# Decoder layer with gated cross-attention on one Trainium2 core: the two products that sum the gates write different partitions of one PSUM bank, and the running maximum reads a copy

## What is computed

```python
itilde = einsum('bsd,hd->bhs', gate_in, Wi_w) + Wi_b
ftilde = einsum('bsd,hd->bhs', gate_in, Wf_w) + Wf_b
csum   = cumsum(log_sigmoid(ftilde), axis=-1)
Fmat   = csum[..., :, None] - csum[..., None, :]
Dtilde = where(tril, Fmat, -inf) + itilde[..., None, :]
max_d  = max(Dtilde, axis=-1)
D      = exp(Dtilde - max_d)
```

## Time and profile before

| | value |
|---|---|
| median of three runs | 1849.2 us (1847.55 to 1849.93) |
| profiled execution, its own time | 1848.03 us |
| its span, first to last instruction | 1846.3 us |
| PE busy | 1772.4 us, 96% of the span |
| PEld busy | 1377.2 us, 75% |
| DVE busy | 1331.0 us, 72% |
| ACT busy | 1151.9 us, 62% |
| POOL busy | 317.5 us, 17% |
| mean granted TensorE clock | 0.982 |

### The profile page before, as it was taken

The page is one execution under the profiler, slowest core; times in us unless marked ns, Lnnn a source line. Parts: engine busy times, 40 slices in busy tenths (PEclk is TensorE's granted clock), DMA queues, the critical chain, the costliest instruction groups (busy, mean ns, idle before and its releaser), DMA issues.

```text
span 1846.3 us, 44235 instructions
## 1 busy us (share of the span) xinstructions
PE 1772.4 (96%) x14172; PEld 1377.2 (75%) x14172; DVE 1331.0 (72%) x3869; ACT 1151.9 (62%) x2634; POOL 317.5 (17%) x301
## 2 busy tenths in 40 slices
PE   5669999999999999999999999999999999999897
PEld 4557777877777787777777777777877777777675
DVE  4677777777777777777777777777777777777752
ACT  1456766666676666667666667666666776666552
POOL 2011211111221111122111212211111221112110
PEclk8889999999999999999999999999999999999998
DMA  5111212221121222112122211212221211221100
GB/s 135 35 39 35 60 37 60 60 59 48 35 60 37 60 60 59 47 37 60 37 60 60 59 38 46 59 38 60 60 58 32 53 49 48 60 60 40 23 15 26
DMA packets 222639, 92.35 MB, mean 50 GB/s; under 512 B 150785, under 2 KB 222082, under 8 KB 222610
## 3 DMA queue, kind: packets, MB, share of 16 engines
q1 hardware_dynamic: 222610, 91.99, 18.9%
HBM read 70.71 MB, written 16.78 MB: 47 GB/s over the span
## 4 chain that ended last, share of the span: by engine, by line
PE 93%; DVE 4%; ACT 1%; issue 1%; DMA 0%; SPq 0%; DVEq 0%; ACTq 0%
PE UA L1460 11%; PE TA L1460 6%; PE UB L1398 6%; PE GT L1460 5%; PE TB L1398 5%; PE PV L1398 5%; PE UA L1423 3%; PE GT L1471 3%; PE TA L1360 3%; PE QQ L1223 3%; PE TA L1398 3%; PE UA L1398 3%; PE DD L1223 2%; PE PV L1506 2%; PE QQ L1491 2%; PE UB L1506 2%
## 5 line engine op out<-in xcount | busy, mean ns | idle before, releaser
L1099 DVE TENSOR_TENSOR C<-qT,QKs 128x512 f32<-128x512 f32 x256 | 178.3, 716 | 181.4 <-ACT qT L759 178.6
L1460 PE MATMUL UA<-W2f,hs_all 128*128 128x256 f32 x1024 | 231.5, 379 | 0.0
L1460 PEld LDWEIGHTS UA<-W2f,hs_all 128*128 128x128 f32 x1024 | 194.4, 190 | 30.5 <-issue 0.2
L618 POOL TENSOR_TENSOR Ng<-HT,gnw_b 128x256 f32<-128x256 f32 x128 | 93.2, 728 | 506.8 <-DVE cden L1112 502.3
L595 POOL TENSOR_TENSOR vc<-vc 128x992 f32<-128x992 f32 x32 | 58.9, 1842 | 632.6 <-DVE ve L871 631.9
L612 POOL TENSOR_TENSOR xg<-x,gnb_b 128x1024 f32<-128x1024 f32 x32 | 75.4, 2356 | 298.2 <-DVE nmx L1065 281.7
L1460 PE MATMUL TA<-W2f,hs_all 128*128 128x256 f32 x512 | 120.8, 379 | 0.0
L1460 PE MATMUL GT<-W2f,hs_all 128*128 128x256 f32 x512 | 115.7, 379 | 0.0
L672 ACT ACTIVATE V<-QQ 128x260 f32<-128x260 f32 x32 | 12.4, 388 | 159.5 <-PE QQ L1255 159.5
L1460 PEld LDWEIGHTS GT<-W2f,hs_all 128*128 128x128 f32 x512 | 94.9, 190 | 11.6
L1460 PEld LDWEIGHTS TA<-W2f,hs_all 128*128 128x128 f32 x512 | 94.9, 190 | 11.3
(11 more groups left out here) (384 smaller groups left out, 5277.8 us busy)
## 6 DMA issues: line engine op xcount, KB each, us to landing
xin<-x SPq DMA_DIRECT2D x32, 512.0 KB, 4.4
xb<-x SPq DMA_DIRECT2D x32, 512.0 KB, 4.1
blocks<-ctx SPq DMA_DIRECT2D x256, 64.0 KB, 2.0
vc<-ctx SPq DMA_DIRECT2D x32, 512.0 KB, 3.6
out<-ot SPq DMA_DIRECT2D x32, 512.0 KB, 3.2
Ev<-xn SPq DMA_DIRECT2D x512, 1.0 KB
hs_all<-L_ffn_W SPq DMA_DIRECT2D x4, 512.0 KB, 9.0
E<-xn SPq DMA_DIRECT2D x128, 16.0 KB
```

The lines of the kernel that those rows point to most:

```text
L618: pool.tensor_tensor(Ng[:, b, :].rearrange("p (k n) -> p k n", k=2), HT[:, b % 2, :, 0:P], gnw_b[:, :].rearrange("p (k n) -> p k n", k=2), ...
L1099: dve.tensor_tensor(C[:, b % 2, :, half], dx[hf].rearrange("p (h i) -> p h i", h=HEADS), QKs[:, b, :, half], ALU.mult)\
L1460: ins = pe.matmul(OB[b][:, 0:D], hs_all[:, k, b * S:(b + 1) * S], W2f[:, k, :], start=(i == 0), stop=(i == KH - 1))
```

## The change

The product with `sel_i` now writes DD[32:64], columns 0 to 127, and the product with `sel_f` still writes DD[0:32], columns 0 to 127: same columns of the bank, different partitions. VectorE's one copy of 32x256 becomes two of 32x128, the first of them from partitions 32 to 63 into partitions 0 to 31 of `acs[:, 1]`. One wait stands behind both. The running maximum reads `acs[:, 1]` in SBUF for both operands.

```diff
-        v_chain = Chain(sem("dve_step"), 42)
+        v_chain = Chain(sem("dve_step"), 43)
...
                 if cross:
                     dve.wait_ge(sel_mm.h, sel_mm.at(it, 1))
-                    link(dve.tensor_copy(acs[:, 0:2, :].rearrange("p a n -> p (a n)"), DD[0:32, 0:2 * P]))
-                    dve.tensor_tensor_scan(acs[:, 2, :], acs[:, 1, :], DD[0:32, P:2 * P], -3e38,
+                    head = v.mark(dve.tensor_copy(acs[:, 1, :], DD[32:64, 0:P]))
+                    tail = v.mark(dve.tensor_copy(acs[:, 0, :], DD[0:32, 0:P]))
+                    dve.wait_ge(v.h, v.upto(head, tail))
+                    dve.tensor_tensor_scan(acs[:, 2, :], acs[:, 1, :], acs[:, 1, :], -3e38,
                                            ALU.max, ALU.max).then_inc(acs_ok.h, 1)
...
                 def sums():
                     pe.wait_ge(csum_ok.h, csum_ok.at(it, 1))
-                    pe.matmul(DD[0:32, P:2 * P], sel_i[:, :], csum[:, :], start=True, stop=True)
+                    pe.matmul(DD[32:64, 0:P], sel_i[:, :], csum[:, :], start=True, stop=True)
                     pe.matmul(DD[0:32, 0:P], sel_f[:, :], csum[:, :], start=True, stop=True).then_inc(sel_mm.h, 1)
```

## The result

The kernel after takes 1841.1 us (median of six executions, 1840.97 to 1841.88), the kernel before, in the same job, 1849.11 us (six, 1847.55 to 1850.1). The ratio is 0.996 with a 95% interval of 0.995 to 0.997. A repeat in a later job gave 1841.8 against 1848.35 us, 0.9965 (0.9951 to 0.9978). That is 6.6 to 8.0 us less; forecast were 6.6 us and 1842.6 us.

A forecast was written before the change was run, and what follows sets the result against it. PE was taken to bound the kernel; 31 steps x 0.21 us plus 0.13 us in step 1 give 6.6 us, so 1849.2 - 6.6 = 1842.6 us. The range was 1841.0 to 1845.9 us.

The forecast's parts named there:

- The bound: Looped steps: PE is busy 1566.82 of 1568.00 us, so shortening PE's work shortens the kernel while other engines keep their slack.
- The sums: PE in `sums()`: two strips overlap, first record to up(4) 0.34 us instead of 0.55, 0.21 us less a step.
- The alternation of the records: PE in `sums()`: the first record of the second product starts some 0.01 us after the first product's first record.
- VectorE's chain: DVE behind the sums: first copy to scan 0.53 us against 0.45, so 0.08 us later, bounds 0.12 earlier to 0.34 later.
- The slack: Looped step, end of scan to qk(0): about 0.43 us, shrinking by 0.08 only, so PE does not wait.
- The port in the loop: DVE and POOL in looped steps: the scan would begin at 898.83, just behind L605's release at about 898.70; nothing paid.
- Step 1: Before qk(0) in the first step: PE does wait for the scan, 1.15 us, so the gain is 0.13 us.
- Rival A: Step 1: the scan loses the port to L605, qk(0) starts 2.24 us later; gain 4.3 us, 1844.9 us; chance 0.18.
- B: PE in `sums()`: strips overlap only in part, three rounds; gain 3.5 us, 1845.7 us; chance 0.07.
- C: PE in `sums()`: the pair goes one behind another, 0 gained on PE; 1849.2 us; chance 0.09.
- D: PE in `sums()`: changing strip drains the array, 0.09 us each time, 2.9 us slower, 1852.1 us; chance 0.04.

The follow-up runs named there:

- Experiment 1: Kernel after with the sel_i product put back to DD[0:32], columns 128 to 255, and VectorE's part kept: 1848.87 us, 0.9998 of before.
- experiment 6: Kernel after with two more copies on VectorE ahead of the scan, into a spare tile: 1849.08 us, 1.0001 of before.
- Experiment 7: Kernel after with one more GpSimd addition right behind L605, both operands in SBUF: 1850.33 us, 1.0007 of before.
- experiment 4: Kernel after with both sums in one product of 128 columns, 64 of them zero: 1839.12 us, 0.9949 of before.
- experiment 5: Kernel after with one more copy on VectorE ahead of the scan, into a spare tile: 1842.14 us, 0.9964 of before.
- experiment 10: Kernel after with both sums in one 128*128 product and the two copies swapped: 1839.35 us, 0.9952 of before.
- experiment 2: Kernel after with sel_f and sel_i in one product of 64 columns, two records instead of four: 1843.14 us, 0.9965 of before.
- experiment 3: Kernel after with a third product in front, into DD[64:96], which nothing reads: 1842.46 us, 0.9966 of before.
- experiment 9: Kernel after once more, unchanged, with more rounds: 1841.8 us, 0.9965 of before.
- experiment 11: Kernel before with both products widened to 128 columns of weights, 96 of them zero, one behind the other: 1845.08 us, 0.9983 of before.
- experiment 8: Control: kernel before with the same extra GpSimd addition as Experiment 7: 1849.19 us, 0.9999 of before.

## Why the prediction was right, point by point

*The bound.* PE, as read from rows 2. Work taken from PE (7.1 us busy) came back almost whole as time. Experiment 1 ties it to the strips.

*The sums.* 0.34 us from first record to up(4) was forecast and is there; 0.21 a step at the sums. Of it 0.197 us remains over a whole step in the first pair of profiles and 0.23 with the second profile of after, so 0.21 was as good as such numbers are. The alternation of the records was forecast too.

*VectorE's chain.* This term was mis-sized. I had taken the copies to start 0.21 us apart, from L1028 and L1029, two operations on the same partitions in SBUF. They start 0.31 apart, and first copy to scan is 0.63 us instead of 0.53. The copy's 280 ns and the scan's 0.41 us were right (282, 279 and 411). The slack was mis-sized too: of the 0.62 us from the end of the scan to qk(0) I had left 0.18 to PE's queue and called 0.43 slack; experiment 6 shows 0.25 as the least, so it was 0.37. The chain is 0.18 us longer than before, not 0.08, and 0.19 us is left. It held, so neither error reached the time in the loop.

*The port in the loop.* Nothing was paid, as forecast: the scan begins at 896.72, L605's record ends at 896.62. The longer chain made this safer, not tighter. Experiment 7 shows what 0.7 us more of GpSimd work there costs (9 us). By the rule cited in the prediction (SBUF — State Buffer, "Who interferes with whom", of the Trainium skill) it is two SBUF inputs that make the difference; the trace agrees, 878 against 407 ns.

*Step 1.* The forecast gain of 0.13 us is not there: 56.08 us against 56.02. The step of the prediction that failed is "PE does wait for the scan", taken as if that wait set the end of step 1. The wait is real (1.3 us at L1425), but PE idles again before the first `pv`, where it waits for DVE's `C`: 3.83 us in after, and in before

```profile
100.32 1.08 PE L1506 MATMUL PV<-C,vc 128*32 128x128 f32 x16 [3.65 <-issue]
```

So DVE's chain behind the scan passes any gain on or takes it away. In after the scan holds the port first, L605's record grows from 2.34 to 2.52 us, and L1030 waits for its end. That addition and the first `pv` (15.47 instead of 15.29 us after the first sums) come 0.17 to 0.18 us later than in before. Even at qk(0) the gain would have been 0.03 us and not 0.13, since the chain is 0.18 us longer.

*Rival A.* It did not happen in after, in either profile, but that was luck: the scan asked 0.05 us ahead of L605 (86.50 and 86.55) and not 0.15 us, as the prediction had it. It happened in experiments 1, 4, 5, 6 and 10 and changed nothing. Its price of 2.24 us was wrong by the same step as above: step 1 took 56.04 to 56.32 us in the five profiles where this scan lost the port, and 56.01 to 56.28 in the five where it went first (experiments 2, 3, 7 and 9 and after). Rivals B, C and D are excluded by the alternating records and by experiment 3.

*The rest.* 6.6 us forecast, 6.1 in the spans, 8.0 and 6.6 in the medians. The first median, 1841.1 us, lies only 0.1 us inside the forecast range (1841.0 to 1845.9). Of the 6.1, 0.6 us between the last two sums is more than the 0.2 that the strips give. The granted clock differs there (column PEclk, third from the right, in 16 us that begin about 10 us before the last sums; before, then after):

```profile
1755.00:1771.00 16.00, 16.00 (x132) 12.06 (x125) 7.02 (x21) 8.80 (x16) 2.37 (x1) 0.87 0.09 29
```

```profile
1750.00:1766.00 16.00, 16.00 (x134) 11.84 (x130) 6.97 (x22) 8.80 (x15) 2.39 (x1) 0.91 0.07 25
```

A part of the stretch ran at the lower of its two levels, 1.2 instead of 2.4 GHz: a shorter part in after. That is worth 16 x 0.04 = 0.6 us, an estimate from the two rows, which would cover the 0.4 us beyond the strips. The same gap took 55.39 us in the second profile of after, 56.14 in experiment 10, and 55.07 in experiment 7, whose looped steps are as long as those of before. So the rest of the 0.6 us is not the strips' doing, and the clock is the likely cause, which no run here isolates. The 8.0 us of the first medians against 6.6 in the repeat has no explanation beyond the spread of single executions, some 3 us for the kernel before.

## What to carry to other kernels

Where the busy time by stretch shows one engine without a gap, price a change by that engine's distance from start to start, and look for the same pattern elsewhere in the kernel to learn what an overlap is worth; here it gave the gain within a few hundredths of a microsecond a step. Small products that can't fill the array go side by side in different partitions of a bank, but if the work around them is full width, padding them with zeros into one full-width product can be better still, because it also spares the change of width; here it was 2 to 2.5 us of 1841. A wait that shows on the bound engine is worth its length only if nothing later in that stage makes the engine wait again.

## What the runs showed of the hardware

- The two records of one f32 product leave room for another strip's between them: first records 0.007 us apart, then the second ones. A third strip put up(4) 0.007 us later (0.349 instead of 0.343 us after the first record, experiment 3).
- From an f32 record with 32 or 64 columns of weights to up(4) with 128, 0.20 us, and up(4)'s weights are loaded only then (before, after, experiment 2). Between f32 records of full width it is 0.11, and 0.03 to up(4) (experiment 11). Avoiding the change of width was worth 0.12 us a step, in experiment 11 against before and in experiment 4 against after (0.04 in the second pair, experiment 10 against 9).
- `tensor_tensor_scan` with both operands in SBUF waits for a GpSimd instruction that is under way and reads SBUF, for 0.47 us in the loop of experiment 7 and up to 2.2 us in step 1; with one operand in PSUM it does not (407 to 409 ns in experiment 8). In step 1 a request 0.03 to 0.05 us ahead of GpSimd's won in five profiles, and L605's record then grew from 2.34 to 2.52 us; one 0.01 us or more behind it lost in five.
- Two VectorE copies from PSUM that read the same 32 partitions start 0.21 us apart, two that read different ones 0.31, in either order. Whether it is the source alone that matters was not tried.
